# Attention stage of a fused transformer kernel: a semaphore raised earlier, the turned maxima split over two steps, the live rows fetched ahead

## What is computed

```
def cond2(x, mask, conditioning, Wq, Wk, Wv, Wo, ...):   # x: (2, 1024, 256), 16 heads of 16
    q, k, v = (proj(Wq), proj(Wk), proj(Wv))             # (2, 16, 1024, 16)
    scores = einsum('bhsd,bhtd->bhst', q, k) * 16 ** -0.5
    scores = where(mask, -inf, scores)                   # mask is True over the valid keys
    attn = softmax(scores, axis=-1)
    out = einsum('bhst,bhtd->bhsd', attn, v)
```

## Time and profile before

| | before |
|---|---|
| median of 3 executions | 1093.75 us (1093.63 to 1093.96) |
| profiled execution, its own time | 1092.6 us |
| span of its instructions | 1090.8 us |
| PE busy | 908.2 us, 83% |
| DVE busy | 766.1 us, 70% |
| ACT busy | 377.2 us, 35% |
| POOL busy | 414.7 us, 38% |

### The profile page before, as it was taken

The page is one execution under the profiler, slowest core; times in us unless marked ns, Lnnn a source line. Parts: engine busy times, 40 slices in busy tenths (PEclk is TensorE's granted clock), DMA queues, the critical chain, the costliest instruction groups (busy, mean ns, idle before and its releaser), DMA issues. The chain is left out here.

```text
span 1090.8 us, 17828 instructions
## 1 busy us (share of the span) xinstructions
PE 908.2 (83%) x5603; PEld 771.2 (71%) x5612; DVE 766.1 (70%) x1473; ACT 377.2 (35%) x709; POOL 414.7 (38%) x480
## 2 busy tenths in 40 slices
PE   3499999999657864988856788877679999999998
PEld 1499999999646653867755655436368888888887
DVE  5788888888458798588655656435557777677776
ACT  4366556665134212122214155455511111111110
POOL 3177877778500340544317322300022323233232
PEclk9599999999979876999977799897789999999999
DMA  8336122341160001400008700000011010000002
GB/s 270 104 121 194 48 68 96 116 163 51 45 200 1 0 1 42 145 1 1 1 0 145 156 1 1 1 1 1 1 30 30 14 29 23 20 29 14 29 0 78
DMA packets 50300, 61.81 MB, mean 57 GB/s; under 512 B 8014, under 2 KB 37768, under 8 KB 50248
## 3 DMA queue, kind: packets, MB, share of 16 engines
q1 hardware_dynamic: 43464, 43.85, 13.0%
q0 software_dynamic: 6336, 17.31, 6.6%
q10 hardware_dynamic: 448, 0.01, 0.0%
HBM read 47.26 MB, written 7.60 MB: 50 GB/s over the span
## 5 line engine op out<-in xcount | busy, mean ns | idle before, releaser
L2248 POOL TENSOR_TENSOR e_hl<-e_h32sb,e_hh 128x512 fp32r<-128x512 f32 x68 | 88.1, 1296 | 289.9 <-DVE e_hh L2272 289.9
L2239 ACT ACTIVATE e_silusb<-psum 128x512 f32<-128x512 f32 x68 | 40.7, 598 | 242.2 <-PE psum L2192 242.2
L2280 DVE SCALAR_TENSOR_TENSOR y<-psum,comb,y 128x256 f32<-128x256 f32 x272 | 112.2, 476 | 0.1
L2269 DVE TENSOR_TENSOR e_h32sb<-psum,e_silusb 128x512 f32<-128x512 f32 x68 | 47.0, 692 | 84.6 <-PE psum L2192 71.3
L443 ACT ACTIVATE e_u<-psum,e_bias 128x256 f32<-128x256 f32 x152 | 63.7, 471 | 96.3 <-PE psum L342 87.5
L2192 PE MATMUL psum<-act_hi,e_w0h 128*128 128x512 f32 x144 | 58.0, 403 | 9.8 <-ACTq L2232 9.8
L1274 POOL TENSOR_TENSOR ff_hl<-ff_h32sb,ff_hh 128x512 fp32r<-128x512 f32 x24 | 34.5, 1439 | 71.1 <-DVE ff_hh L1309 71.1
L1836 DVE TENSOR_REDUCE at_mn<-psum 128x4 f32<-128x512 f32 x64 | 42.3, 687 | 24.7 <-PE psum L1533 18.8
L2192 PE MATMUL psum<-act_hi,e_w0l 128*128 128x512 f32 x144 | 57.2, 397 | 0.0
L2192 PE MATMUL psum<-act_lo,e_w0h 128*128 128x512 f32 x144 | 57.1, 397 | 0.0
L352 PE MATMUL psum<-e_w3h,e_h2h 128*128 (+1 forms) x160 | 47.1, 295 | 8.6 <-issue 8.2
(11 more groups left out here) (503 smaller groups left out, 3228.2 us busy)
## 6 DMA issues: line engine op xcount, KB each, us to landing
e_raw<-in_W SPq DMA_DIRECT2D x16, 512.0 KB, 7.0
e_raw<-in_W SPq DMA_DIRECT2D x8, 1024.0 KB, 5.8
y<-in_x SPq DMA_DIRECT2D x4, 512.0 KB, 9.8
v_tok<-in_xT SPq DMA_DIRECT2D x4, 512.0 KB, 8.2
y<-y_rows SPq DMA_DIRECT2D x4, 512.0 KB, 6.9
v_tok<-y_rows SPq DMA_DIRECT2D x4, 512.0 KB, 7.8
v_tok<-in_x SPq DMA_DIRECT2D x4, 512.0 KB, 8.7
e_raw<-in_w_gate SPq DMA_DIRECT2D x16, 128.0 KB, 2.2
```

What stands on the lines that cost most here:

```text
L2239: act.activation(sl_sb[:, s % 2, :], ps[s % 2][:, :], ACT.Silu).then_inc(sil, 1)
L2248: pool.tensor_tensor(hh[1][:, s % HS, :], h32[:, s % 2, :], hh[0][:, s % HS, :], ALU.subtract).then_inc(hsp, 1)
L2269: dve.tensor_tensor(h32[:, s % 2, :], ps[2 + s % 2][:, :], sl_sb[:, s % 2, :], ALU.mult).then_inc(h32d, 1)
L2280: dve.scalar_tensor_tensor(out=y[:, i, :], in0=ps[4 + j][:, 0:D], scalar=comb[:, i, bass.ds(2 * t + out_s // G, 1)], in1=y[:, i, :], op0=A ...
```

## The change

1. POOL raises `moved` by two right behind its own memsets, ahead of the transfers into the stacks.
2. `x32` and `xt` (the live rows and their two halves) have buffers of their own. Tile 0 is prepared in the head: ACT copies it behind the fifth query group, PE transposes it into bank 3 behind the seventh, ACT and DVE write its halves there. In the loop, tile `j + 1` is prepared in value steps 12 and 13, whether there is such a tile or not; the loop no longer begins with this.
3. ACT's first instruction in the stage is an exponential of one column, which puts the load of the exponential's table there.
4. `turn_maximum` and both `maximum_out` take one half each. In the lead, half 0 is turned behind score 17 and half 1 behind score 19 (both stood behind 19). In steps 2, 6 and 10, half 0 stands at `k` = 1 and half 1 at `k` = 2 on PE and ACT, one `k` later on DVE; the factor's exponential moves to `k` = 3.
5. `LEAD` is 22 and not 24.
6. `normalise` of units 0 to 2 stands behind steps 6, 10 and 14 and not 5, 9 and 13.

```diff
@@ -1387,15 +1387,15 @@
...
-    LEAD = NA + 8
+    LEAD = NA + 6
...
-    xt = [v[:, :, :].rearrange("p k (b t) -> p k b t", b=B) for v in wq]
+    xt = [sbl(f"at_xt{h}", [P, KC, B, P], F32R) for h in "hl"]
...
-    x32 = spare_raw[:, 2 * GT:3 * GT].rearrange("p (b d) -> p b d", b=B)
+    x32 = sbl("at_x32", [P, B, D])
@@ -1467,6 +1467,14 @@
 
     @block.tensor
     def _(pe):
+        def turn_tile(bank, j):
+            pe.wait_ge(xcp, j + 1)
+            for k in range(KC):
+                for b in range(B):
+                    last = pe.transpose(bank[:, (k * B + b) * P:(k * B + b + 1) * P],
+                                        x32[:, b, k * P:(k + 1) * P], ident[:, :])
+            last.then_inc(xps, 1)
...
+            if u == 2 * NU - 2:
+                turn_tile(ps[3], 0)
@@ -1539,18 +1541,18 @@
...
-        def turn_maximum(j, unit, n_added):
-
-            pe.wait_ge(nm_set, j * NU + unit + 1)
...
-            for h in range(2):
-                if h:
...
+        def turn_maximum(j, unit, h, n_added):
+
+            if h:
+                turned_out(j * NU + unit, 1)
+            else:
+                pe.wait_ge(nm_set, j * NU + unit + 1)
+                pe.wait_ge(added, j * NBT + n_added + 1)
+            for n in range(HB):
+                last = pe.matmul(ps[7][CP:NK, n * P:(n + 1) * P],
+                                 nm[:, unit % 2, h * HB + n, :, :].rearrange("p h e -> p (h e)"), ident[:, :],
+                                 start=True, stop=True)
+            last.then_inc(nm_ps, 1)
@@ -1595,7 +1597,6 @@
...
             pe.wait_ge(added, j * NBT + 1)
-            turn_tile(j)
@@ -1608,9 +1609,10 @@
...
-                if a == NA + 3:
+                if a == NA + 1:
                     pe.wait_ge(vb_set, j + 1)
-                    turn_maximum(j, 0, 0)
+                if a in (NA + 1, NA + 3):
+                    turn_maximum(j, 0, (a - NA) // 2, 0)
@@ -1620,23 +1622,41 @@
...
                     if k == 1 and t:
                         values(j, t - 1)
-                    if k == 1 and t % NV == NV - 2 and unit + 1 < NU:
-                        turn_maximum(j, unit + 1, t - 1)
+                    if k in (1, 2) and t % NV == NV - 2 and unit + 1 < NU:
+                        turn_maximum(j, unit + 1, k - 1, t - 1)
                     if k == 3 and t:
                         if t % NV == NV - 2 and unit + 1 < NU:
                             turned_out(j * NU + unit + 1, 2)
                         turn_back(j, t - 1)
+                if t == NBT - 3:
+                    pe.wait_ge(red, (j + 1) * NAT + 3)
+                    turn_tile(ps[0], j + 1)
...
     @block.scalar
     def _(act):
+        def copy_tile(j):
+            jt = tile_at(act, j)
+            act.activation(x32[:, :, :].unsqueeze(2), y_tok[:, :, :].rearrange("p (b q) d -> p b q d", b=B)
+                           [:, :, bass.ds(jt, 1), :], ACT.Copy).then_inc(xcp, 1)
+
+        def tile_hi(bank, j):
+            act.wait_ge(xps, j + 1)
+            act.activation(xt[0][:, :, :, :].rearrange("p k b t -> p (k b t)"), bank, ACT.Copy).then_inc(xhi, 1)
+
+        act.activation(idle[:, :], ident[:, 0:1], ACT.Exp)
         flat = acc[:, :, :, :, :].rearrange("p b u h e -> p (b u h e)")
         act.activation(flat, ident[:, 0:1].to_broadcast([P, B * QT * NH * (HD + 1)]), ACT.Copy, scale=0.0).then_inc(zeroed, 1)
...
             b, m, g = u // (2 * KC), u // 2 % KC, u // (2 * KC) * 2 + u % 2
             act.wait_ge(qps, u + 1)
             act.activation(q_hi[:, m, g * GT:(g + 1) * GT].bitcast(F32R), ps[u % 3], ACT.Copy).then_inc(qhi, 1)
+            if u == 2 * NU - 4:
+                act.wait_ge(counted, 1)
+                copy_tile(0)
+            if u == 2 * NU - 2:
+                tile_hi(ps[3], 0)
@@ -1663,10 +1683,9 @@
...
-        def maximum_out(j, unit):
-            for h in range(2):
-                act.wait_ge(nm_ps, (j * NU + unit) * 2 + h + 1)
-                act.activation(maximum_rows(unit, 0, h), turned_rows, ACT.Copy).then_inc(nm_act, 1)
+        def maximum_out(j, unit, h):
+            act.wait_ge(nm_ps, (j * NU + unit) * 2 + h + 1)
+            act.activation(maximum_rows(unit, 0, h), turned_rows, ACT.Copy).then_inc(nm_act, 1)
@@ -1674,12 +1693,7 @@
 
         n = live_tiles(act)
         with act.Fori(0, n) as j:
-            jt = tile_at(act, j)
             act.wait_ge(added, j * NBT + 1)
-            act.activation(x32[:, :, :].unsqueeze(2), y_tok[:, :, :].rearrange("p (b q) d -> p b q d", b=B)
-                           [:, :, bass.ds(jt, 1), :], ACT.Copy).then_inc(xcp, 1)
-            act.wait_ge(xps, j + 1)
-            act.activation(xt[0][:, :, :, :].rearrange("p k b t -> p (k b t)"), ps[7], ACT.Copy).then_inc(xhi, 1)
@@ -1696,9 +1711,14 @@
                     exponentials(j, t, k)
                     if k == 2 and t:
                         values_out(j, t - 1)
-                    if k == 1 and t % NV == NV - 2 and unit + 1 < NU:
-                        maximum_out(j, unit + 1)
+                    if k in (1, 2) and t % NV == NV - 2 and unit + 1 < NU:
+                        maximum_out(j, unit + 1, k - 1)
+                    if k == 3 and t % NV == NV - 2 and unit + 1 < NU:
                         factor(j, unit + 1)
+                if t == NBT - 4:
+                    copy_tile(j + 1)
+                if t == NBT - 3:
+                    tile_hi(ps[0], j + 1)
@@ -1709,6 +1729,8 @@
...
+        pool.wait_ge(cset, 5)
+        pool.nop().then_inc(moved, 2)
...
-        pool.nop().then_inc(moved, 2)
@@ -1773,6 +1793,11 @@
...
+        def tile_lo(bank, j):
+            dve.wait_ge(xhi, j + 1)
+            dve.tensor_tensor(xt[1][:, :, :, :].rearrange("p k b t -> p (k b t)"), bank,
+                              xt[0][:, :, :, :].rearrange("p k b t -> p (k b t)"), ALU.subtract).then_inc(xsp, 1)
@@ -1812,6 +1837,8 @@
...
             query_lo(5 + copy)
+            if copy == 1:
+                tile_lo(ps[3], 0)
@@ -1846,10 +1873,9 @@
...
+        def maximum_out(j, unit, h):
+            dve.wait_ge(nm_act, (j * NU + unit) * 2 + h + 1 + 3)
+            dve.tensor_copy(maximum_rows(unit, 1, h), maximum_rows(unit, 0, h)).then_inc(nm_dve, 1)
@@ -1886,8 +1909,8 @@
...
-                if a == NA + 3:
-                    maximum_out(j, 0)
+                if a in (NA + 3, LEAD - 1):
+                    maximum_out(j, 0, int(a == LEAD - 1))
@@ -1895,10 +1918,12 @@
...
-                    if k == 1 and t % NV == NV - 2 and t // NV + 1 < NU:
-                        maximum_out(j, t // NV + 1)
-                if t % NV == 1 and t > 1:
+                    if k in (2, 3) and t % NV == NV - 2 and t // NV + 1 < NU:
+                        maximum_out(j, t // NV + 1, k - 2)
+                if t % NV == 2 and t > 2:
                     normalise(j, t // NV - 1)
+                if t == NBT - 3:
+                    tile_lo(ps[0], j + 1)
```

More of the change, by code:

```diff
@@ L1419, in stage_attention @@
                 n_live, live_at = sbl("at_nlive", [P, 1], I32), sbl("at_liveat", [P, QT + 1], I32)
-                rc, idle = sbl("at_rc", [P, QT, HC]), sbl("at_idle", [P, 1])
+                rc, idle, done = sbl("at_rc", [P, QT, HC]), sbl("at_idle", [P, 1]), sbl("at_done", [P, 1])
                 block = st.enter_context(nc.Block())
@@ L1482, in _ @@
                             pe.matmul(ps[7][:, 0:QT], one[:, :], keys[:, :], start=True, stop=True).then_inc(cnt_ps, 1)
-                    def turn_tile(j):
-                        pe.wait_ge(xcp, j + 1)
-                        for k in range(KC):
-                            for b in range(B):
-                                last = pe.transpose(ps[7][:, (k * B + b) * P:(k * B + b + 1) * P],
-                                                    x32[:, b, k * P:(k + 1) * P], ident[:, :])
-                        last.then_inc(xps, 1)
+                        if u == 2 * NU - 2:
+                            turn_tile(ps[3], 0)
                     def stack_keys(*pairs):
@@ L1540, in turned_out @@
                         pe.wait_ge(nm_act, g * 2 + halves + 3)
-                    def turn_maximum(j, unit, n_added):
-                        pe.wait_ge(nm_set, j * NU + unit + 1)
-                        pe.wait_ge(added, j * NBT + n_added + 1)
-                        for h in range(2):
-                            if h:
-                                turned_out(j * NU + unit, 1)
-                            for n in range(HB):
-                                last = pe.matmul(ps[7][CP:NK, n * P:(n + 1) * P],
-                                                 nm[:, unit % 2, h * HB + n, :, :].rearrange("p h e -> p (h e)"), ident[:, :],
-                                                 start=True, stop=True)
-                            last.then_inc(nm_ps, 1)
+                    def turn_maximum(j, unit, h, n_added):
[9 more added lines that the diff above has]
+                        last.then_inc(nm_ps, 1)
                     def turned_scores(j, t, k):
```

(16 more changed lines are left out.)

## The result

| | before | after |
|---|---|---|
| median | 1093.69 us (1092.84 to 1093.96, 4 executions) | 1075.98 us (1075.31 to 1076.54, 4 executions) |
| profiled execution, own time | 1092.6 us | 1076.54 us |
| its span | 1090.8 us | 1074.8 us |
| DVE busy | 766.1 us | 768.5 us |

The ratio is 0.9843, with a 95% interval of 0.9818 to 0.9868, so the kernel is 1.6% faster, clear of the noise. In a later series, beside other kernels, it was 0.9843 again (0.9829 to 0.9856; 1077.16 against 1094.55 us).

The account below looks back on a forecast made before the run. The prediction took hand-overs between PE, ACT and DVE in one stage, with four standstills, to bound the kernel. Its terms sum to -15.4 us: profiled execution 1092.6 to 1077.2, median 1078.4, range 1075 to 1085, chance 0.62.

Parts of the forecast that it names:

- The four places of standstill: Where PE, ACT and DVE all stand still: the head, first maxima, a maximum's turn, and value steps 2, 6 and 10.
- The head, -2.7: Stage start to PE's first key matmul: live rows prepared earlier, less the table load's delay; 2.7 us sooner, bounds 2.0 to 4.5.
- the rival that rests on it: A drain of about 1.38 us comes ahead of the table load in the head: 1.4 us more, 1079.8; chance 0.03.
- The first maxima, -4.7: First scores: early `moved` wins PE's 3.22 us wait, and an earlier clock rise 1.5 us; together 4.7 us.
- The rival of cold first scores: PE stays at 1.2 GHz through the first scores, so the 1.5 us is lost and more: 1081; chance 0.10.
- The lead's turn, -1.5: Unit 0's maximum, turned in halves among scores: first turned score 5.95 us after the negated maximum, not 7.52; 1.5 us less.
- Steps 2, 6 and 10, -5.4: Value steps that turn a maximum: 8.99, 10.46 and 11.12 us each fall to 8.4, gaining 0.6, 2.1 and 2.7 us.
- Step 11, -2.0: Value step 11, at a low clock before (6.24 us against 4.28), was expected to hold the clock: 2.0 us less.
- The rival of a fall in step 10 all the same: Clock still falls in step 10; step 11 gives nothing and step 10 about 1.3 us less: 1081.7; chance 0.15.
- The tail, +0.9: Steps 12 and 13 prepare a tile that doesn't exist: transposes 0.66 us, ACT 0.2; 0.9 us more.
- No change: Exponentials must wait for the last transfer into the stacks, so an earlier lead only waits longer: 1093 us; chance 0.05.
- slower: Finer interleaving keeps PE below what holds the clock, running value steps at 1.2 GHz; twelve cold steps give 1104; chance 0.05.

Follow-up runs that it names:

- the kernel with the late load: The kernel after with the one-column exponential, and so the table load, behind the last query copy on ACT instead of ahead of the zeroing: 1076.19 us, ratio 0.9848.
- the semaphore alone: The kernel before with only `moved` raised early by POOL, ahead of its transfers into the stacks: 1085.3 us, ratio 0.9935.

## Why the prediction was right, and where not

The four places of standstill were the right ones, and the sum for the stage, 15.4, was 15.65. The profiled execution was forecast at 1077.2 us and came at 1076.54; the median was forecast at 1078.4 and came at 1075.98. That the sum is nearer than its terms is luck in part: the head was 0.3 us better and the tail 0.5, and steps 2, 6 and 10 together 0.6 worse. By its steps:

- **The head, -2.7: -3.0**, by the way described. The table load moved the zeroing's end from 3.8 to 5.2 us behind the stage's start, 1.4. The load begins 1.01 us after PE's release, where in the kernel with the late load the zeroing begins 1.02 us after the same release, and the next instruction starts 1.29 us after the load's start. The drain that the Trainium skill, "ScalarE: Activation LUTs", What ACT_TABLE_LOAD costs, puts beside the load is thus not borne out, and the rival that rests on it falls. The forecast's lower bound, 2.0, doesn't follow from the 2.10 us that it names, which would have left 0.6; the register load cost ACT 0.60 us of idle time ahead of its copy (586.64), and DVE none.
- **The first maxima, -4.7: -4.7** (7.73 less the head's 3.0), the semaphore alone 4.6. That the two are coupled, with the head worth nothing while POOL's copies bind, was not in the prediction; the sum came out because both were changed at once. Over the 3.22 us of PE's wait 1.5 are left, which was the clock's share as taken; the two stretches show the clock higher, and no run splits the sum further. The rival of cold first scores holds for scores 0 to 3 only.
- **The lead's turn, -1.5: -1.5.** T to the first turned score went from 7.48 to 5.96.
- **Steps 2, 6 and 10, -5.4: -4.8.** They end at 8.5 to 8.6 and not 8.4. Four kernels with `normalise` moved show that the split and `LEAD` simply add. The one with `LEAD` 24 and one turn is before with `normalise` moved, so its head and its semaphore are the old ones too; the steps without a turn are as long in it as in the others to 0.03 us, so this is counted as nothing:

| steps 2, 6, 10 | one turn | split |
|---|---|---|
| `LEAD` 24 | 9.02, 9.04, 8.08 | 7.78, 7.80, 6.85 |
| `LEAD` 22 | 9.88, 9.75, 9.74 | 8.63, 8.52, 8.51 |

The split takes 1.24 off each step (3.7 in all). `LEAD` 22 costs 0.86, 0.71 and 1.66 (3.2). `normalise` gives the rest, by the run on the kernel before: 1.41 in step 6, 2.94 in step 10 and 2.06 in step 11, 6.4.

- **The step that failed** is the sentence "Two scores went from the lead into step 10, where PE has room". Its price on the turn was in the terms (half 0 at +3.55), but it was told as if it bought the lead something. T to the first turned score is 5.96 with either, because PE idles there. Without it the change would have given 3.2 us more.
- **Step 11, -2.0: -2.0, for one of two reasons that each suffice.** The prediction laid it on shorter idle pieces, 0.7 us and not 1.1. With the halves turned together, and pieces of 0.55, 1.11 and 1.47, the clock held too, because the move of `normalise` had taken away the wait of 1.62 that came first; the prediction didn't see this. With `normalise` in its old place, the turn split and `LEAD` at 22, it held as well (waits of 1.79 and 0.56). The rival of a fall in step 10 all the same is seen in no profile of a kernel with the split or with the moved `normalise`, most of which have one profile.
- **The tail, +0.9: +0.4.** The four transposes show, 0.43; ACT's and DVE's parts are hidden.
- **No change and slower** fell: no exponential waited on a transfer, and the granted clock was 1.00 from 611 us to the end of the stage.

## What to carry to other kernels

Where the waits of two engines end at one instruction, the one that ends last sets what the other is worth: the head's 3 us were worth nothing while the semaphore was late, and the semaphore 4.6 us by itself. Ask of each piece of work that is moved what was idle where it stood: two scores cost nothing in a lead where PE waits, and 3.2 us in the steps that they went to. On an engine that everybody waits for, long work of no urgency (`normalise`, 2 us) belongs behind the short work that another engine waits for (`add`, 0.43 us), and in the kernel before that one order was worth 6.4 us, half of it clock. In the kernel after, where the split turn held the clock already, it was worth 2.4.

## What the runs showed of the hardware

- **Behind which waits the clock fell.** In step 10 the granted clock fell behind waits of 1.62 and 1.11 us with 1.0 us of work between, in before and in before with the early semaphore. It held behind 1.26 and 1.10 in before's step 6, behind 1.79 and 0.56 and behind 0.55, 1.11 and 1.47 in step 10 of two variants, and when step 10's waits were filled with matmuls that nobody reads; the filler gave 3.25 us. Ahead of step 0 one wait of 1.67 us was followed by a fall (late load) and held in another kernel at the same place (after with the old `normalise`). What tells these two apart is open, so a fall behind one wait can't be forecast from its length here.
- **A table load costs its own length.** In the profiles of before and after, ACT goes from one instruction through a load into the next ten times each without a wait: the load starts 0.02 us behind the instruction ahead of it, takes 1.28 us, and the next starts 1.29 us after the load's start.
- **The clock's course differs between executions, also of one kernel.** In the head it rose 4.3 us into the stage in most profiles and 7.3 in three (late load, `LEAD` 24, and before with `normalise` moved, whose head is that of before), and T moved by up to 2 us with it. The two profiles of the kernel after agree within 0.1 us. But single executions of a kernel don't all have the same mean granted clock: those of before have 0.907 to 0.919, and the two shortest of them, 1087.0 and 1088.7 us, the two highest. After with the old `normalise` has 0.922 in its profiled execution of 1076.98 us and 0.919 in the three near 1079.8. The Trainium skill, "TensorE: Matmul & The Clock Gate", Part 1, has the ramp lie elsewhere from run to run of one kernel; the two profiles of after don't show that, the mean clocks agree with it, and one profile of each variant can't tell whether its text or the execution set the rise. For an experiment this means that a difference of 2 us at T between two variants can be clock. Step lengths at full clock repeat to 0.03 us and can be subtracted.
